# Spiking stage of a one-core kernel: ScalarE's row work split around each projection's sign, TensorE's transposes placed ahead of its projection

## What is computed

```python
x = x + L0_conv(ln_c(x), ...)              # spectral convolution
t = t + L0_ffn(ln_t(t))                    # a shift of 8-bit values coded in the channels
x = x + L1_conv(ln_c(x), ...)              # spiking attention: T=4, B=32, N=64 is the view of ln_c(x)
    # branch(i): y = bn(x @ lin_w[i].T + lin_b[i]); s = lif(y, 1.0)
    # lif: v += (xt - v)/2; s = (v >= v_th); v *= 1 - s      (a chain over the leading axis)
    # o = lif((q @ k.T * 0.125) @ v, 0.5);  lif(bn(o @ lin_w[3].T + lin_b[3]), 1.0)
t = t + L1_ffn(ln_t(t), ...)               # mixture of 8 experts, top 2
```

## Time and profile before

| | us |
|---|---|
| median of 3 runs (1256.29 to 1259.03) | 1257.32 |
| the profiled execution | 1256.02 |
| its span (first to last instruction) | 1254.1 |
| busy in the span: PE, DVE, ACT, POOL | 982.3, 827.8, 626.2, 565.3 |
| mean granted TensorE clock, of full speed | 0.864 |

### The profile page before, as it was taken

How to read it: one execution, slowest core, us unless ns; L and a number is a source line. 1 busy time by engine, 2 the same in 40 slices (tenths; PEclk the granted TensorE clock), 3 DMA queues, 4 the chain that set the end, 5 groups by cost and what they waited for, 6 DMA issues and landing times. The chain is left out here.

```text
span 1254.1 us, 23605 instructions
## 1 busy us (share of the span) xinstructions
PE 982.3 (78%) x6627; PEld 824.6 (66%) x6628; DVE 827.8 (66%) x2676; ACT 626.2 (50%) x1334; POOL 565.3 (45%) x730
## 2 busy tenths in 40 slices
PE   9958848766668677767776541399999999999997
PEld 7848826544456465555555530288888888888886
DVE  7724435755869889798865472166666666666665
ACT  3434414476596877877762430144444444444443
POOL 3310001112223667675664777355545554555454
PEclk9979969977787888787886555699999999999999
DMA  9569587900010110000000000111111111111110
GB/s 371 253 185 292 179 229 179 214 19 20 20 51 20 35 38 25 12 29 14 33 16 21 30 25 34 46 41 42 45 48 43 47 50 50 46 42 49 49 40 2
DMA packets 83330, 93.56 MB, mean 75 GB/s; under 512 B 7708, under 2 KB 75548, under 8 KB 79929
## 3 DMA queue, kind: packets, MB, share of 16 engines
q1 hardware_dynamic: 74201, 75.33, 20.3%
q0 software_dynamic: 9056, 17.33, 4.2%
HBM read 56.07 MB, written 38.32 MB: 75 GB/s over the span
## 5 line engine op out<-in xcount | busy, mean ns | idle before, releaser
L1738 POOL DMA_INDIRECT out_dram<-res,index x155 | 154.8, 999 | 215.7 <-DVE res L1804 187.8
L1847 ACT ACTIVATE sil<-ps_h 128x512 f32<-128x512 f32 x155 | 92.6, 597 | 253.0 <-PE ps_h L1899 253.0
L1769 DVE TENSOR_TENSOR act_rows<-ps_h,sil 128x512 f32<-128x512 f32 x155 | 107.3, 692 | 131.8 <-ACT sil L1847 131.8
L1918 PE MATMUL ps_y<-r_raw,aT 128*128 x1240 | 163.8, 275 | 0.0
L1918 PEld LDWEIGHTS ps_y<-r_raw,aT 128*128 128x128 f32 x1240 | 150.7, 192 | 0.1
L159 POOL DMA_INDIRECT slots<-x_sb,r_pos x128 | 131.4, 1027 | 42.1 <-issue 37.1
L1897 PE MATMUL ps_h<-r_raw,uTh 128*128 x310 | 136.5, 440 | 1.8 <-DVE uTl L1763 1.6
L1898 PE MATMUL ps_h<-r_raw,uTh 128*128 x310 | 123.6, 399 | 0.0
L1899 PE MATMUL ps_h<-r_raw,uTl 128*128 x310 | 121.9, 393 | 0.0
L1089 PE MATMUL ps_q<-wqkv,zT 128*128 128x256 f32 x256 | 114.5, 540 | 0.0
L1201 POOL TENSOR_TENSOR x_sb<-x_sb,sy 128x256 f32<-128x256 f32 x64 | 43.0, 672 | 146.5 <-ACT sy L1347 146.4
(11 more groups left out here) (239 smaller groups left out, 2368.3 us busy)
## 6 DMA issues: line engine op xcount, KB each, us to landing
wc<-in_mixing_weights SPq DMA_DIRECT2D x8, 2048.0 KB, 14.1
slots<-zero SPq DMA_DIRECT2D x4, 2652.0 KB, 23.2
pay<-slots SPq DMA_DIRECT2D x39, 272.0 KB, 2.8
x_sb<-in_token_rows SPq DMA_DIRECT2D x8, 1088.0 KB, 5.7
sblk<-coefficients SPq DMA_DIRECT2D x16, 256.0 KB, 5.9
mixed<-mo SPq DMA_DIRECT2D x16, 256.0 KB, 7.5
gin<-mixed SPq DMA_DIRECT2D x16, 256.0 KB, 14.2
r_raw<-in_L_ffn_W SPq DMA_DIRECT2D x8, 508.0 KB
```

The source lines that it names most:

```text
L1738: nc.gpsimd.indirect_dma_start(out_rows, bass.IndirectOffsetOnAxis(at, 0), res[:, m % RES, :], None, bounds_check=TOKENS - 1, oob_is_err=F ...
L1769: nc.vector.tensor_tensor(act_rows[:, k], ps_h[:, k, :, DFF:], sil[:, k], ALU.mult).then_inc(s_act, 1)
L1847: nc.scalar.activation(sil[:, k], ps_h[:, k, :, 0:DFF], ACT.Silu).then_inc(s_sil, 1)
L1918: ins = nc.tensor.matmul(dst, aT[:, k, (2 * e + h) * P:(2 * e + h + 1) * P], raw[:, 4 + h, col], start=(h == 0), stop=(h == 1))
```

## The change

ScalarE's `behind` is split. A new `ahead(i, b)` stands, from round 1 on, before `sign_projected`; the rest stays behind `spike_output`. TensorE's transposes move out of `beside` into `turns(i, b)`, from round 1 on right behind `attend` and so ahead of `project_out` and `project`. The `route_turn`s, two in slot 4 and two in slot 5, become one in slot 4, two in slot 5 and one in slot 6; `route_rank` and `route_logits` stay behind the projection. No instruction is added or taken away; in round 0 the order stays as it was but for the sizes of the parts.

```diff
                 for g in range(1, G):
                     z_rows(act, 0, g)
 
-                def behind(i, b):
+                def ahead(i, b):
 
                     n, r = i + 1, i - 2
                     if b in (0, 1, 2) and i < NP2:
                         major(act, i, b + 1)
                     if b == 0 and n < NP2:
-                        u_rows(act, n, 0, 10)
+                        u_rows(act, n, 0, 4)
+                    if b == 1 and n < NP2:
+                        u_rows(act, n, 10, 14)
+                    if b == 2 and n < NP2:
+                        x_rows(act, n, 4, 8)
+                    if b == 3 and n < NP2:
+                        x_rows(act, n, 14, NT)
+                    if b == 3 and r >= 0:
+                        route_rows(act, r, 0)
+                    if b == 4 and r >= 0:
+                        route_major(act, r, 0)
+                        route_rows(act, r, 2)
+                    if b == 5 and r >= 0:
+                        route_major(act, r, 1)
+                        route_major(act, r, 2)
+                    if b == 6 and r >= 0:
+                        route_major(act, r, 3)
+                    if b == LAST and n < NP2:
+                        z_rows(act, n, 2)
+                        major(act, n, 0)
+
+                def behind(i, b):
+
+                    n, r = i + 1, i - 2
+                    if b == 0 and n < NP2:
+                        u_rows(act, n, 4, 10)
                     if b == 0 and r >= 1:
                         exponential(act, r - 1)
                     if b == 1 and n < NP2:
-                        u_rows(act, n, 10, NT)
+                        u_rows(act, n, 14, NT)
                         x_rows(act, n, 0, 4)
                     if b == 2 and n < NP2:
-                        x_rows(act, n, 4, 13)
-                    if b == 3 and n < NP2:
-                        x_rows(act, n, 13, NT)
+                        x_rows(act, n, 8, 14)
                     if b == 3 and r >= 0:
-                        route_rows(act, r, 0)
+                        route_rows(act, r, 1)
                     if b == 4 and r >= 0:
-                        route_rows(act, r, 1)
-                        route_major(act, r, 0)
-                        route_rows(act, r, 2)
-                        route_major(act, r, 1)
-                    if b == 5 and r >= 0:
                         route_rows(act, r, 3)
-                        route_major(act, r, 2)
-                        route_major(act, r, 3)
                     if b == 6 and n < NP2:
                         z_rows(act, n, 0)
                         z_rows(act, n, 1)
                     if b == LAST and n < NP2:
-                        z_rows(act, n, 2)
-                        major(act, n, 0)
                         z_rows(act, n, 3)
 
                 for i in range(NP2 + 1):
...
                             sign_attended(act, i - 1, b)
                         if k >= 1:
                             sign_output(act, *divmod(k - 1, B))
+                        if i:
+                            ahead(i, b)
                         if i < NP2:
                             sign_projected(act, i, b)
                         if k >= 1:
                             spike_output(act, *divmod(k - 1, B))
+                        if i == 0:
+                            ahead(i, b)
                         behind(i, b)
                 sign_output(act, NP2 - 1, LAST)
                 spike_output(act, NP2 - 1, LAST)
...
 
                 def beside(i, b):
 
-                    n, r = i + 1, i - 2
+                    r = i - 2
                     if b == 0 and r >= 1:
                         route_rank(pe, r - 1)
+                    if b == 6 and r >= 0:
+                        route_logits(pe, r)
+
+                def turns(i, b):
+
+                    n, r = i + 1, i - 2
                     if b in (0, 1, 2) and i < NP2:
                         turn(pe, i, b + 1)
-                    if b in (4, 5) and r >= 0:
-                        route_turn(pe, r, 2 * b - 8)
-                        route_turn(pe, r, 2 * b - 7)
-                    if b == 6 and r >= 0:
-                        route_logits(pe, r)
+                    if b in TURN_SLOTS and r >= 0:
+                        for g in TURN_SLOTS[b]:
+                            route_turn(pe, r, g)
                     if b == LAST and n < NP2:
                         turn(pe, n, 0)
+
+                TURN_SLOTS = {4: (0,), 5: (1, 2), 6: (3,)}
 
                 for i in range(NP2 + 1):
                     for b in range(B):
...
                             pe.wait_ge(s_ca, 4 * NP2)
                         if k >= 0:
                             attend(pe, i - 1, b)
+                        if i:
+                            turns(i, b)
                         if k >= 1:
                             project_out(pe, *divmod(k - 1, B))
                         if i < NP2:
...
                         if b in (5, 7) and i < NP2:
                             key_values(pe, i, b // 2 - 2)
                         beside(i, b)
+                        if i == 0:
+                            turns(i, b)
                 project_out(pe, NP2 - 1, LAST)
                 route_rank(pe, NP2 - 2)
                 for g in range(G):
```

## The result

| | before | after |
|---|---|---|
| median of the runs, us | 1256.80 (1255.31 to 1259.03, 4 runs) | 1277.06 (1274.61 to 1280.20, 4 runs) |
| ratio | | 1.0174, 95% interval 1.0145 to 1.0203 |
| profiled execution, us | 1256.02 | 1280.20 |

The change makes the kernel slower, by 20.3 us where 10 were forecast; 1277.06 lies above the forecast's 1252 to 1276. The profiled executions lie 24.2 us apart. 6.1 of these lie ahead of round 0 and 1.3 in it. The part ahead of round 0 ends (at the first sign) between 254.4 and 261.3 us in the fourteen kernels of this study, which all share its code; so 16.8 us are left for the rounds that the change touches. The other 3.5 of the 20.3 are not placed: one execution of each kernel is read here.

What follows compares the result with a forecast made beforehand. No engine is full; a chain of waits once round the four engines each round bounds the kernel. Terms 4 + 8.4 - 3 + 0.8 = +10.2 on 1256.02 give 1266.2, median forecast 1267 us, range 1252 to 1276.

Steps and rivals of the forecast that it cites:

- Link 2: From the rank's end to sign 1: 5.02 falls to 3.4, gain 1.6; near 0 if the clock is low.
- Link 3: From sign 1 to sign 2, ScalarE full: 5.88 rises to 6.1, loss 0.2.
- Link 4: From sign 2 to reset 3: routed rows waiting for route_scale ahead of sign 3 raise 7.7 to 9.5, loss 1.8.
- Link 5: From reset 3 to the first z row, VectorE the limit: stays 22.1.
- Link 6: From the first z row to sign 7: 3.80 rises to 5.8 to 7.2, the largest loss.
- Link 1: From the choice's end to the end of TensorE's rank matmuls: 2.76 in the mean, kept unchanged.
- Link 7: From sign 7 through VectorE's last spikes to the choice's end: 7.4.
- Rounds 1 and 2: No rank ahead, so no gain at sign 1; +4 us together, bounds +3.4 to +6.3.
- Rounds 7 and 8: Round 7, without next-group rows: -3 (-5.4 to -2); round 8, without projection: +0.8 (-1 to +2).
- Faster: TensorE at full clock: Rival: transposes in idle time keep TensorE at its upper clock, sum -4, time 1253; chance 0.21.
- Much slower: Rival: z row to sign 7 at 7.2 in all rounds, round 7 at low clock: +18, 1275; chance 0.06.

Runs made afterwards that it cites:

- the filler's kernel: The changed kernel plus matmuls nobody reads: 24 ahead of the rank and 8 ahead of slot 7's transposes; 1272.24 us, ratio 1.0160.
- Slot 7 alone: The kernel before with only slot 7's z rows and copy ahead of sign 7 and transposes ahead of project(7), rounds 1 to 6; 1278.53 us, 1.0179.
- ScalarE's half behind sign 7 again: The changed kernel with ScalarE's third z rows and copy behind sign 7, TensorE's transposes still ahead of project(7); 1273.82 us, 1.0142.
- slots 0 to 2 alone: The kernel before with the change in slots 0 to 2 only, from round 1; 1255.76 us, 0.9998.
- The last combined version: The kernel before with changed slots 0 to 2 from round 3, and changed slots 4 to 6 in rounds 7 and 8; 1246.18 us, 0.9935.
- both parts behind: The changed kernel with the first routed rows behind sign 3 and slot 7's rows, copy and transposes taken back; 1254.99 us, 1.0000.
- rows 0 behind: The changed kernel with only the first four routed rows put back behind sign 3; 1275.51 us, 1.0153.

## Why the prediction was right in direction and short in size

- **Link 2**, sign 1 3.4 behind the rank, gain 1.6: 3.38 and 1.63. Right, and on its condition: the projection behind the rank took 1.97 at a granted clock of 1.00 in each of rounds 3 to 6, so the case of a low clock, with a gain near 0, did not come up. **Link 3**, +0.2: +0.26. **Link 4**, +1.8 with 1.8 of waiting at reset 3: +1.68 with 1.71. **Link 5** stays: 22.36 to 22.39 (the 22.1 was round 5's own). These four steps held.
- **Link 6** is the term that failed. The prediction gave 5.8 to 7.2 and took the lower end, as the mean clock of 0.83 "is the upper level for two thirds of the time". It was 6.97 on the mean, +2.59. A mean over the rounds was the wrong number for one place in them: `project(7)` was granted 0.50 to 0.69. The change did not bring that low clock, it put it on the path. Before, `project(7)` had 0.52 to 0.62 in three of the four rounds, but mostly began ahead of the z rows; now it begins 3.46 behind the first. The upper end, worked out from low-clock rows as 1.6 + 1.9 + 3.7 = 7.2, is what came in three rounds of four to within 0.1 (7.13, 7.23 and 7.23). The low clock was visible in the earlier trace rows, in that very slot. The lower end was also set too low: 5.84 at full clock came as 6.06 in the filler's kernel.
- **Link 1** was held at its 2.76; it became 3.63, +0.87. The prediction said that an earlier `project(n, 0)` "is not on the path" and left it there. It had not asked what that projection did in its old place: it filled TensorE's time up to `chosen`, where before the rank found 0.17 to 1.89 us of idle time ahead of it in rounds 3 to 6. Gone from there, it leaves 3.5 to 4.4, and the rank was granted 0.50 to 0.58 in each round. Slot 7 alone on the kernel before does the same (3.76); with ScalarE's half behind sign 7 again, and that projection in its old place, the 16 matmuls are back at 1.79 to 2.12.
- **Link 7**, 7.4: 7.41. A round grew by 0.87 - 1.63 + 0.26 + 1.68 + 0.03 + 2.59 + 0.25 = 4.05 by its links, 16.2 for four. Of the 7.8 that were missing, 4 x 0.87 = 3.5 are link 1, and another 3.5 are link 6: the 8.4 taken stands 0.3 a round over the lower end, so it held link 6 at 6.1, and 4 x (6.97 - 6.1) = 3.5. The last 0.8 is mainly link 5, where the sum took round 5's 22.1 for the mean: round 5's links and 2.76 add up to 54.6, and were set beside a mean round of 55.26.
- **The bounds.** The bounds of the four parts add up to +4.0 to +19.3, and not to the +3.8 to +18 of the prediction: 1261 to 1277.
- **Rounds 1 and 2**: +5.9 inside the bounds of +3.4 to +6.3. The runs with rounds 0 to 2 wholly in the old order (147.8 to 148.7) against those with the changed slots 0 to 2 there (151.4 to 156.8) show that the order itself costs there. That link 2 gains nothing in these rounds was right; that slots 0 to 2 alone cost about 2 us in rounds 1 and 2 was not seen.
- **Rounds 7 and 8**: -4.9 and -0.4 inside their bounds; the 15.02 between signs 4 and 6 became 8.38, forecast 7.8 to 11.2. The last combined version, which has that part in rounds 7 and 8, repeats it (8.39).
- **The rivals.** "Faster: TensorE at full clock" fell: the clock dropped from 0.83 to 0.75. Behind it stood the Trainium skill, "TensorE: Matmul & The Clock Gate", section "Part 1: The HAM clock gate", by which activity releases the clock. The rank agrees with that rule and speaks against the use made of it: the change adds no matmul (1220 in rounds 3 to 6 in both kernels), it moves them, and TensorE's idle time ahead of the rank grows from 0.2 to 1.9 us to 3.5 to 4.4. Where the rest of the mean clock's fall lies, and why slot 7 is mostly at the lower level in both kernels, stays open: with both parts behind, the mean is 0.77 as well. "Much slower", link 6 at 7.2 in all rounds, 1275, had 6 in 100 and was nearest. Its mechanism, link 6 at low clock, held in three rounds of four. It had no term for link 1.

## What to carry to other kernels

Before a producer's work is moved ahead of a recurrence's step in an in-order queue, list what its **first** instruction waits for: if that ends later than the step's own operand, the step inherits the wait, and everything queued behind it too. Ask as well what the moved work did in its old place: a projection that filled a gap ahead of a critical group of matmuls was worth 0.9 us a round, nearly all of it by the clock. Price a step at the clock that rows show in its own place, and not at the mean of the stage, the more so where the change brings onto the path what ran beside it; and apply such an order only in the rounds in which it pays, as the last combined version does, at 0.9935.

## What the runs showed of the hardware

- The rank's 16 matmuls take 1.79 us at full clock and 3.38 at half. In rounds 3 to 6 idle times of 3.5 to 4.6 us ahead of it always gave 3.04 to 3.38 (the changed kernel, rows 0 behind, slot 7 alone); with 1.04 or less all four of the last combined version took 1.79. Between and below, the idle time ahead does not settle it: 2.56 us gave 2.97 and 3.04 us gave 1.79 in the filler's kernel, and the earlier trace rows hold a 2.68 that stands behind only 0.23 of idle time.
- The mean clock and the time need not go together: 0.77 with both parts behind and 54.77 a round, 0.83 before and 55.26. Off the path a low clock cost nothing, as `project(7)` of round 5 before shows.
- The part ahead of round 0, the same code in all, ended between 254.4 and 261.3 us. One profiled execution against another can't resolve 5 us of the whole; rounds and links can be compared, as they repeat.
- VectorE's last instruction of the choice took 0.62 or 0.63 us in most rounds and 1.06 to 1.17 in 36 of its 112 instances in the fourteen kernels (after: ahead of rounds 5 and 7; before, ahead of rounds 3 to 7: in none). In all 36 GpSimd's add (L1201) lay beside it for 0.5 us or more. Of the other 76 three had that add beside them, and there the add took 0.99 to 1.00, against 0.67 in most. So wherever the two met, one of them was stretched; below is the meeting ahead of round 5. It is 0.5 us in link 7 of two rounds of the kernel after. No run was made to part the two.

```profile
533.36 1.17 DVE L981 TENSOR_TENSOR chosen<-pair_no,pair 128x448 bf16<-128x448 f32 x1
...
533.99 1.05 POOL L1201 TENSOR_TENSOR x_sb<-x_sb,sy 128x256 f32<-128x256 f32 x1
```
